# The order inside the loop of a decoder's second attention: banks, GpSimd's residual, counted places and slots

## What is computed

```python
x = _layernorm(x + linear_attention(x, w_qkv, w_out, b_out))        # elu+1 kernel, 16 heads of 16
x = _layernorm(x + cross_attention(x, ctx_1024, ...))               # 77 context rows, one head
x = _layernorm(x + ffn(x, ...))

def ffn(hidden):                       # hidden read as (S=256, B=16, H=256)
    ln1 = _layernorm(hidden, ln1_weight, ln1_bias)
    q, k, v = split(ln1 @ qkv_weight.T)                # 16 heads, 4 key heads, attention over the first axis,
    probs = softmax(causal(q @ k.T * hd ** -0.5))      # which in this layout has 16 entries
    h = hidden + (probs @ v) @ proj_weight.T
    x = _layernorm(h, ln2_weight, ln2_bias)
    gate = softmax(x @ router_weight.T)                # 8 experts, the two best of each token
    moe = sum over the two of gate * (gelu(x @ w1[e]) @ w2[e])
    return h + moe
```

## Time and profile before

| | us |
|---|---|
| median of 3 runs (lowest, highest) | 772.32 (772.12, 772.46) |
| the profiled execution | 771.22 |
| its span | 769.4 |
| TensorE matmuls busy | 651.1 (85%) |
| VectorE busy | 528.0 (69%) |
| ScalarE busy | 388.7 (51%) |
| GpSimd busy | 311.3 (40%) |
| mean granted TensorE clock, share of full | 0.926 |

### The profile page before, as it was taken

The page is one execution under the profiler, slowest core; times in us unless marked ns, Lnnn a source line. Parts: engine busy times, 40 slices in busy tenths (PEclk is TensorE's granted clock), DMA queues, the critical chain, the costliest instruction groups (busy, mean ns, idle before and its releaser), DMA issues.

```text
span 769.4 us, 19214 instructions
## 1 busy us (share of the span) xinstructions
PE 651.1 (85%) x5188; PEld 543.0 (71%) x5189; DVE 528.0 (69%) x1846; ACT 388.7 (51%) x921; POOL 311.3 (40%) x439
## 2 busy tenths in 40 slices
PE   6799999999844889898876329999999999999790
PEld 4679898998723667676655217888888888888340
DVE  2368778878834668787875747777777777777373
ACT  1446565666436566555343614555555555555044
POOL 0246777777550022655668732222222222222132
PEclk9999999999976999989976559999999999999996
DMA  6343443443310000111111322222222222221584
GB/s 202 98 129 100 142 121 101 142 132 83 95 26 16 2 3 2 51 50 58 57 50 68 114 90 65 69 70 81 69 73 78 69 79 73 69 82 56 167 355 154
DMA packets 47709, 68.13 MB, mean 89 GB/s; under 512 B 10576, under 2 KB 34512, under 8 KB 47664
## 3 DMA queue, kind: packets, MB, share of 16 engines
q1 hardware_dynamic: 39080, 46.01, 20.3%
q0 software_dynamic: 6480, 17.87, 6.2%
q10 hardware_dynamic: 2104, 3.68, 1.5%
HBM read 40.21 MB, written 23.12 MB: 82 GB/s over the span
## 4 chain that ended last, share of the span: by engine, by line
PE 33%; issue 28%; DVE 3%; DMA 2%; SPq 1%; ACT 1%; ACTq 0%; DVEq 0%; POOLq 0%
PE half_bank L145 9%; PE half_bank L147 9%; PE half_bank L146 9%; PE half_bank L1920 5%; PE half_bank L1901 2%; DVE region_en_small L155 1%; DMA region_y_rows<-results 1%; DVE region_y_rows L1664 1%; ACT all_w L1678 1%; SPq L1708 1%; DVE all_w L921 1%; DMA results<-all_w_qkv,ex_home 0%; SPq L1707 0%; DVE region_en_small L158 0%; DMA all_xh<-dispatched 0%
## 5 line engine op out<-in xcount | busy, mean ns | idle before, releaser
L1739 POOL DMA_INDIRECT results<-all_w_qkv,ex_home x71 | 68.2, 960 | 201.5 <-DVE all_w_qkv L1864 177.1
L1772 ACT ACTIVATE region_hid_hi<-half_bank 128x256 fp32r<-128x256 f32 x142 | 46.7, 381 | 81.0 <-PE half_bank L1920 81.0
L969 POOL DMA_INDIRECT dispatched<-all_xh,all_slot_u x64 | 67.9, 1062 | 40.2 <-DVE all_slot_u L1341 23.3
L145 PE MATMUL half_bank<-region_w_hi,region_hid_hi 128*128 x284 | 81.4, 287 | 2.5 <-DVE region_hid_lo L1856 2.5
L146 PE MATMUL half_bank<-all_w,region_hid_hi 128*128 x284 | 79.7, 281 | 0.0
L147 PE MATMUL half_bank<-region_w_hi,region_hid_lo 128*128 x284 | 79.5, 280 | 0.0
L1864 DVE TENSOR_SCALAR all_w_qkv<-half_bank,ex_gate 128x256 f32<-128x256 f32 x71 | 34.3, 484 | 49.1 <-PE half_bank L147 48.5
L1759 ACT ACTIVATE all_xh<-half_bank,all_ln_b,all_ln_w 128x128 f32<-128x128 f32 x142 | 57.7, 467 | 18.8 <-PE half_bank L1901 18.8
L145 PE MATMUL half_bank<-region_w_hi,region_x_hi 128*128 x142 | 62.5, 440 | 0.5 <-DVE region_x_lo L1849 0.5
L145 PEld LDWEIGHTS half_bank<-region_w_hi,region_hid_hi 128*128 128x128 f32 x284 | 53.2, 187 | 13.4 <-issue 10.4
L1766 ACT ACTIVATE all_w_proj<-half_bank 128x512 f32<-128x512 f32 x71 | 42.5, 599 | 39.1 <-PE half_bank L147 39.1
(11 more groups left out here) (247 smaller groups left out, 1805.6 us busy)
## 6 DMA issues: line engine op xcount, KB each, us to landing
all_xh<-dispatched SPq DMA_DIRECT2D x71, 130.5 KB
all_w<-in_moe_w_dram SPq DMA_DIRECT2D x32, 256.0 KB, 3.1
region_y_rows<-results SPq DMA_DIRECT2D x12, 512.0 KB, 10.4
all_resid<-at_x SPq DMA_DIRECT2D x32, 128.5 KB
shared_x_t<-in_x_t_dram SPq DMA_DIRECT2D x16, 256.0 KB, 4.2
at_x_tok<-in_x_dram SPq DMA_DIRECT2D x16, 256.0 KB, 4.3
region_y_rows<-results SPq DMA_DIRECT2D x8, 256.0 KB, 9.5
out_dram<-all_w ACTq DMA_DIRECT2D x4, 512.0 KB
```

Source lines behind the costliest of these rows:

```text
L145: nc.tensor.matmul(out, a_hi, b_hi, start=(start and i == 0), stop=False)
L969: nc.gpsimd.indirect_dma_start(out=dram["dispatched"], out_offset=bass.IndirectOffsetOnAxis(ap=keep["slot_u"][g % SENDS][:, u, k:k + 1], a ...
L1739: nc.gpsimd.indirect_dma_start(out=dram["results"], out_offset=bass.IndirectOffsetOnAxis(ap=home[par][:, 0:1], axis=0), in_=ym[par], in_of ...
L1772: nc.scalar.activation(hid_hi[par][:, cs, :], p_t[half], ACT.Copy).then_inc(s["hid_high"], 1)
```

## The change

Four edits in the second attention. The list `order` deals the banks out with the queries ahead of "kv", and "x" ahead of "p"; TensorE's order of filling stays. `send_rows` takes numbers of single scatters (0 to 7) in place of tiles. GpSimd's turn n was: six scatters of group n-3, `root(n-1)`, `residual(n-1)`, two scatters. It is now: five scatters, `residual(n-1)`, one, `root(n-1)`, two. `count_places(n-2)` moves from the end of TensorE's turn into the middle of `attended(n)`, for all turns but the last. `route_slots(n-2)` stands ahead of the two `add(n)` in all turns, where it stood behind them in all but the last.

```diff
--- before.py
+++ after.py
@@ -962,10 +962,10 @@
                 moe["tensor"](pe)
 
 
-def send_rows(nc, dram, keep, g, tiles):
-
-    for u in tiles:
-        for k in range(2):
+def send_rows(nc, dram, keep, g, numbers):
+
+    for number in numbers:
+        for u, k in (divmod(number, 2),):
             nc.gpsimd.indirect_dma_start(
                 out=dram["dispatched"], out_offset=bass.IndirectOffsetOnAxis(ap=keep["slot_u"][g % SENDS][:, u, k:k + 1], axis=0),
                 in_=keep["xh2"][g % SENDS][:, u, :], in_offset=None).then_inc(keep["scattered"][g % SENDS], 16)
@@ -1018,7 +1018,7 @@
 
     order = []
     for n in range(-2, GROUPS + 1):
-        for what, g, parts in (("s", n, 2), ("kv", n + 1, 1), ("q", n + 1, 2), ("p", n, 2), ("x", n + 2, 2), ("o", n, 2),
+        for what, g, parts in (("s", n, 2), ("q", n + 1, 2), ("kv", n + 1, 1), ("x", n + 2, 2), ("p", n, 2), ("o", n, 2),
                                ("v", n + 1, 2), ("a", n, 2), ("h", n - 1, 2)):
             order += [(what, g, i) for i in range(parts) if there(g)]
     bank_of = Banks(m, "bank", keep["banks"][:7], order)
@@ -1061,9 +1061,9 @@
             steps.chain(nc.gpsimd.tensor_tensor(mean[:, :], mv_h[:, :, 0], rstd_h[:, :], ALU.mult))
             nc.gpsimd.tensor_scalar(shift_h[:, :], mean[:, :], -1.0, None, ALU.mult).then_inc(s["h_rstd"], 1)
 
-        def scatter(g, tiles):
+        def scatter(g, numbers):
             wait_apart(pool, s["slots_ready"], g + 1)
-            send_rows(nc, dram, keep, g, tiles)
+            send_rows(nc, dram, keep, g, numbers)
 
         def residual(g):
             pool.wait_ge(s["h_ready"], 2 * g + 2)
@@ -1073,16 +1073,18 @@
 
         for n in range(1, GROUPS):
             if there(n - 3):
-                scatter(n - 3, range(0, 3))
-            root(n - 1)
+                scatter(n - 3, range(0, 5))
             residual(n - 1)
             if there(n - 3):
-                scatter(n - 3, range(3, NI))
-        scatter(GROUPS - 3, range(0, 3))
+                scatter(n - 3, range(5, 6))
+            root(n - 1)
+            if there(n - 3):
+                scatter(n - 3, range(6, 2 * NI))
+        scatter(GROUPS - 3, range(0, 6))
         root(GROUPS - 1)
-        scatter(GROUPS - 3, range(3, NI))
-        scatter(GROUPS - 2, range(NI))
-        scatter(GROUPS - 1, range(NI))
+        scatter(GROUPS - 3, range(6, 2 * NI))
+        scatter(GROUPS - 2, range(2 * NI))
+        scatter(GROUPS - 1, range(2 * NI))
         residual(GROUPS - 1)
 
     def scalar_program(act):
@@ -1360,13 +1362,10 @@
                 second_statistics(n - 1)
             if there(n - 2):
                 route_pick(n - 2)
-                if n == GROUPS - 1:
-                    route_slots(n - 2)
+                route_slots(n - 2)
             if there(n):
                 add(n, 0)
                 add(n, 1)
-            if there(n - 2) and n < GROUPS - 1:
-                route_slots(n - 2)
         second_statistics(GROUPS - 1)
         route_pick(GROUPS - 2)
         route_slots(GROUPS - 2)
@@ -1469,6 +1468,8 @@
                 bank_of.wait_read(pe, "o", g, y)
             fills = [bank_of.fill(pe, "a", g, i) for i in range(2)]
             for y in range(2):
+                if y == 1 and there(g - 2) and g < GROUPS - 1:
+                    count_places(g - 2)
                 for r in range(REP):
                     for i, (bank, full) in enumerate(fills):
                         half = slice(HALF * i, HALF * (i + 1))
@@ -1520,8 +1521,6 @@
                 attended(n)
             if there(n - 1):
                 turn_rows(n - 1, "h", s["xh2_ready"], xh2[(n - 1) % SENDS])
-            if there(n - 2) and not last:
-                count_places(n - 2)
         route(GROUPS - 2)
         count_places(GROUPS - 2)
         turn_rows(GROUPS - 1, "h", s["xh2_ready"], xh2[(GROUPS - 1) % SENDS])
```

## The result

The changed kernel took 790.58 us (median of 4 runs, 789.31 to 794.48), the kernel before on the same chip 772.22 (4 runs, 771.66 to 772.46): a ratio of 1.0247, 95% interval 1.021 to 1.0284. It is slower by 18 us, where 763.7 was forecast and 771.0 was the end of the range. The profiled execution took 794.48 us (span 792.7), the slowest of the four.

The account below looks back on a forecast made before the run. The second attention was taken as bound by a ring of engines, with late results in turns with scatters. Four such turns -7.7 us, group 2's -0.75, first -1.1, last +0.9 sum to -8.65: 763.7 us, 8-in-10 range 758.5 to 771.

Parts of the forecast that it names:

- the lateness: Router and transposes in turns with scatters: results about 2 us late beside the scatters' transfers, expected to go.
- the sum: Second attention: four turns with scatters -7.7 us, group 2's -0.75, first -1.1, last +0.9; together -8.65 us.
- this rival: Late results move with the scatters onto rows, scores and first projection: scores 2.4 us late, 775 us in all; chance 0.13.
- The ring: Second attention's loop VectorE, GpSimd, ScalarE, TensorE, VectorE, taken to bound a turn: 18.48 us before, 18.8 after, without the residual's meeting.
- The wait in the middle of the projection: TensorE waits there for VectorE's picks before counting places: about 0.7 us idle, adding 0.45 us to the ring.
- a sign against it: In the middle of the projection: the count waiting over 1.5 us would show the forecast wrong.
- The meeting of residual and products: GpSimd's residual, about 4 us into the next turn, falls on VectorE's two products: 0.9 us a turn on the ring.
- The bound of 2.4: Upper bound in us a turn for residual against VectorE's products, if both products wait a whole instruction.
- The banks: New order of banks in the second attention: 1.1 us gained in the first turn, 0 on the ring from group 1 on.
- Slots, picks, outputs: Slots off the ring (1.07 us a turn), picks at shortest times 177 and 191 ns, no L1258 wait ahead of outputs.
- The granted clock: TensorE's clock, fallen in three turns with scatters (0.92, 0.84, 0.85), should stay up once the lateness goes.
- the fourth case: Rival: lateness moves by half, or the mid-projection wait grows 1.5 us; turns of 21.2 us, 770.5 to 772 us; chance 0.11.

Follow-up runs that it names:

- the last run: Changed kernel with scatters held until the scores, six ahead of the residual, count behind the projection, on a first-kind chip (before 771.36 us): 769.35 us, 0.9972.
- the held kernel: Changed kernel with GpSimd waiting for group n's scores before the five scatters: 758.36 us (0.9961), 756.8 us (0.995) and 759.46 us (0.9968), all on second-kind chips.
- held_end: The held kernel with places counted behind the whole projection instead of in its middle: 763.05 us, 1.0035 of the kernel before.
- held_end6: held_end with a sixth scatter ahead of GpSimd's residual: 755.19 us, 0.9908 of the kernel before.
- those two probes: Kernel before plus, in two turns, ten GpSimd additions, or five indirect transfers of 32 rows, beside the scores: 759.96 and 763.26 us.
- SyncE's probe: Kernel before plus five plain DMAs of 128 rows of 1044 bytes by SyncE in each of two turns, GpSimd doing nothing: 773.8 us.

## Why the prediction was wrong, point by point

- **The reading of the lateness was right, the conclusion was not.** "The router's small matmuls and the transposes behind them are slow while the scatters' transfers are under way" holds on the first kind of chip: with the scatters gone from there the "remote" idle time went, and in the last run it came back with them. The router and transposes did run on time with the scatters gone. The step that failed is what the sum made of that: "the lateness of about 2 us goes", with nothing put down for it at the scatters' new place. The eight scatters still ran in every turn, and lay now beside the one stretch where TensorE issues most: 64 matmuls and 64 weight loads in 1.16 us. The forecast held against this rival that "those parts ran on time beside two scatters", and gave it 0.13. Five in a row were another matter.
- **Its price was mis-sized.** The rival's 2.4 us was about the lateness of 16 router matmuls and 8 transposes, carried over to 64 matmuls; it measured 5.4 to 6.4 us a turn. It also came in group 2's turn, because the slots that are ready earlier let the first group's scatters start in it: the sum had given that turn a gain of 0.75 for being free of them, and it lost 4.5. The turns of groups 2 to 6 grew by 20.6 us together; less 1.15 of the first that is the 19.4 of the stage.
- **The ring was right.** 18.8 us were worked out; the held kernel ran at 18.85, with 19.2 once in each trace and 19.4 once in one of three. The wait in the middle of the projection was forecast at 0.7 us and is 0.7 to 1.0 there. Its price was right as well: with the count behind the projection the turns are 18.5, 0.35 less, where the forecast has 0.45 less 0.13. In the changed kernel on the first chip TensorE waited 1.6 us there once, which the forecast counted as a sign against it.
- **The meeting of residual and products** was on neither side where it was put. On the first chip it didn't occur, for VectorE waited for the scores in that time. On the second kind it did, and 0.9 us was too little: the product itself took 1.2 to 1.7 us longer, and the turns of the changed kernel with scatters are 1.1 to 3.0 us over the ring of 18.85, 1.9 on average (the longest lost clock too, 0.84). The forecast let residual and product take turns instruction by instruction; the rows show the product waiting for both. The bound of 2.4 was nearest.
- **The gain to be had** was taken from a chip of the first kind, 2 us a turn of lateness. On the second kind a turn has 0.7 us to win in all (19.5 to 18.8), and a meeting of 1.9 makes it a loss: 1.0069.
- **The banks** were right: 1.1 us in the first turn, nothing in the others, and in the whole change given back in group 3's turn.
- **Slots, picks, outputs** were right: picks at 189 and 192 ns, no L1258 ahead of the outputs, slots off the ring.
- **The granted clock** was to stay up. In the held kernel's rows above it does (1.00); in the changed kernel on the first chip it fell in three of four (0.95, 0.90, 0.91), behind the starved scores. That it falls because TensorE stood idle isn't shown: with the banks alone it was 0.91 in two turns without such idle time.
- **Three slips in the working** change nothing of this: the turn without scatters has 8.4 us less on GpSimd, not 7; the picks would end at 303.40, not 303.35; and the fourth case's four turns of 21.2 are 1.7 us under the measured ones, not 1, which makes it 769.7 and not 770.5.

What is shown: that scatters beside the scores are enough for the loss on the first kind (five indirect transfers add 5.0 us a turn to the kernel before, SyncE's none, and with the scatters held back the scores have no holes), and that the meeting costs turns on the second kind (held_end against held_end6, and the long products of the changed kernel itself). What stays open: by what way GpSimd's indirect transfers make TensorE's work late. Volume and plain writing are out. That they delay TensorE's supply of instructions fits "issue" and the dense scores, but was only argued, and it doesn't explain the 2.7 to 6.9 us between the end of TensorE's records and VectorE's start; a late signal or late results would. The profile also lists DMA transfers of the kind "instruction" (one, of 0.02 MB, from 330 to 345 us of the changed kernel's trace); whether the scatters hold these up wasn't tested. Whether GpSimd's being busy alone would do it, or fewer rows would help, isn't known, as those two probes met a chip that isn't affected. Nor is it known why chips differ.

## What to carry to other kernels

A stall that goes with a piece of work isn't gone when the work is moved; look at what now lies beside it, and count the instructions per microsecond there. Two engines that lock each other out want a place in the order with room, not one that just misses: here one scatter of 1.27 us more or less ahead of the residual decided 3.5 to 4 us a turn. And the size of a stall read on one chip can be nought on another, so a small gain that rests on it should be timed on several.

## What the runs showed of the hardware

- On one kind of chip, 64 small matmuls beside GpSimd's indirect transfers of 128 rows took 7.0 us instead of 1.16, with holes of 0.4 to 1.1 us between groups of mostly 1 to 6 matmuls. In the probes five such transfers made VectorE wait 5.7 us for them, with 20-byte rows as with 1044-byte ones, and SyncE's plain transfers of the same data 0.72, as without any. On three chips of the other kind no such hole was seen.
- An indirect transfer kept GpSimd busy for 0.96 us, with 20-byte rows as with 1044-byte ones, and for 0.87 us with 32 rows instead of 128; the first of a row took up to 1.25 us.
- The Trainium skill's page SBUF — State Buffer, section "SBUF: two separate sides", has it that a transfer can't slow an engine. SyncE's probe agrees (0.72 us of idle time, as without it). With five and with eleven indirect ones in a row VectorE waited 5.70 and 12.13 us for TensorE's scores; no row shows that this comes by way of SBUF's ports, so it doesn't speak against the rule.
- A VectorE product of 0.69 us with both inputs in SBUF took 1.84 to 3.31 us beside two GpSimd additions of 1.16 each and ended only after both, even where its record starts 0.44 us ahead of the first of them (332.06 and 332.50 in held_end).
